# Gate and up weights turned by the host instead of folded on the chip, their low-rank term as one more product, and query blocks as 64-row products

## What is computed

```python
xn = layernorm(x)                                  # 2048 tokens, 512 wide
# attention: 32 heads of 16, 8 groups of keys and values, causal
s = softmax(mask(q @ k.T) / 4) @ v @ Wo + bo       # q = xn @ Wq, k, v = xn @ Wkv
# gated layer with low-rank terms (rank 16), hidden width 1376
gate = xn @ gate_w.T + (xn @ gate_a.T) @ gate_b.T
up   = xn @ up_w.T   + (xn @ up_a.T)   @ up_b.T
hid  = silu(gate) * up
y    = hid @ down_w.T + (hid @ down_a.T) @ down_b.T
out  = x + s * silu(y)
```

## Time and profile before

| | us |
|---|---|
| median of three runs | 944.62 |
| the profiled execution | 946.66 |
| its span, first to last instruction | 944.9 |
| TensorE busy | 896.9 (95%) |
| VectorE busy | 583.7 (62%) |
| ScalarE busy | 488.5 (52%) |
| GpSimd busy | 314.7 (33%) |
| mean granted TensorE clock | 0.984 |
| DMA | 129.20 MB, mean 137 GB/s |

### The profile page before, as it was taken

One profiled execution on the slowest core, in us unless ns is written; L12 is line 12 of the kernel. 1 busy time (PEld: TensorE's weight loads), 2 busy tenths in 40 slices (PEclk: granted clock), 3 DMA queues, 4 the chain that ended last, 5 costly groups with the idle time before them and its releaser, 6 DMA issues.

```text
span 944.9 us, 21107 instructions
## 1 busy us (share of the span) xinstructions
PE 896.9 (95%) x8075; PEld 633.1 (67%) x8075; DVE 583.7 (62%) x1688; ACT 488.5 (52%) x990; POOL 314.7 (33%) x316
## 2 busy tenths in 40 slices
PE   3898999999999999999999999999889999999997
PEld 3765667676766666667676766554667777777885
DVE  7756666666666666665656565777666666650136
ACT  3522656565555656565656565656445454546211
POOL 4231235252525343525252434441121313121133
PEclk9978999999999999999999999998999999999999
DMA  9466343333333342424242434347565647415774
GB/s 290 165 193 192 92 129 97 122 97 114 108 115 110 97 130 83 137 71 148 58 138 84 126 99 121 100 142 204 155 183 156 171 124 194 137 53 171 205 216 142
DMA packets 142946, 129.20 MB, mean 137 GB/s; under 512 B 36176, under 2 KB 104368, under 8 KB 142624
## 3 DMA queue, kind: packets, MB, share of 16 engines
q1 hardware_dynamic: 142848, 127.87, 45.6%
HBM read 74.07 MB, written 53.22 MB: 135 GB/s over the span
## 4 chain that ended last, share of the span: by engine, by line
PE 88%; DVE 5%; DMA 3%; ACT 2%; issue 2%; SPq 1%; DVEq 0%
PE bank L1011 27%; PE o L1182 14%; PE bank L1045 12%; PE s L1146 10%; PE st L1165 8%; PE bank L286 4%; PE bank L287 4%; PE bank L288 4%; DMA ring<-in_L_attn_x 2%; PE bank L986 1%; PE bank L990 1%; DMA q<-scratch_q 1%; DVE junk L1723 1%; PE s L1153 1%; ACT prob L1442 1%
## 5 line engine op out<-in xcount | busy, mean ns | idle before, releaser
L1442 ACT ACTIVATE prob<-st 128x512 f32<-128x512 f32 (+1 forms) x640 | 323.2, 554 | 263.4 <-PE st L1165 262.8
L1723 DVE CUSTOM_DVE_ANT_0 junk<-s,mask 128x128 bf16<-128x128 f32 (+3 forms) x512 | 229.1, 487 | 69.7 <-PE s L1146 67.9
L1726 DVE TENSOR_REDUCE part_max<-s 128x1 f32<-128x512 f32 x256 | 164.0, 682 | 116.3 <-PE s L1146 116.1
L1146 PE MATMUL s<-k,q 64*128 64x512 f32 (+3 forms) x768 | 150.7, 379 | 12.2 <-DVE part_max L1723 4.6
L567 POOL TENSOR_SCALAR_AFFINE_SELECT prob<-prob 128x512 f32<-128x512 f32 x128 | 81.8, 652 | 225.8 <-ACT prob L1442 224.3
L1011 PE MATMUL bank<-x_hi,w_hi 64*128 64x512 f32 (+1 forms) x704 | 150.2, 412 | 2.4 <-DVE hid L1564 1.1
L1182 PE MATMUL o<-prob,v 128*32 128x512 f32 (+3 forms) x1536 | 145.4, 497 | 0.0
L1011 PE MATMUL bank<-x_lo,w_hi 64*128 64x512 f32 (+1 forms) x704 | 142.8, 391 | 0.0
L1011 PE MATMUL bank<-x_hi,w_lo 64*128 64x512 f32 (+1 forms) x704 | 142.1, 389 | 0.0
L1165 PE MATMUL st<-q,k 64*128 64x512 f32 (+3 forms) x768 | 130.7, 356 | 2.3 <-ACT prob L1442 1.8
L1146 PEld LDWEIGHTS s<-k,q 64*128 64x128 f32 x768 | 79.1, 188 | 53.6 <-DVE part_max L1723 24.4
(11 more groups left out here) (148 smaller groups left out, 1089.0 us busy)
## 6 DMA issues: line engine op xcount, KB each, us to landing
late_context_hid_in<-scratch_hid SPq DMA_DIRECT2D x16, 1408.0 KB, 7.2
q<-scratch_q SPq DMA_DIRECT2D x60, 200.0 KB
scratch_hid<-tanh_hid_hi SPq DMA_DIRECT2D x40, 256.0 KB, 2.1
scratch_hid<-hid_lo SPq DMA_DIRECT2D x40, 256.0 KB, 2.4
scratch_o<-o_sb SPq DMA_DIRECT2D x32, 256.0 KB
scratch_q<-proj_hi SPq DMA_DIRECT2D x30, 256.0 KB
k<-scratch_k SPq DMA_DIRECT2D x30, 192.0 KB
x_again<-in_L_attn_x SPq DMA_DIRECT2D x16, 256.0 KB, 4.4
```

Source lines behind the costliest of these rows:

```text
L1146: pe.matmul(sb_[(p + odd) % S_BANKS][:, 0:wd], q[half, g % 2, h // 2, qt * P:(qt + 1) * P], k[half, g % 2, k0:k0 + wd], start=True, stop=T ...
L1442: nc.scalar.activation(prob[:, job % 3, h, 0:JOB_COLS[j]], st[at % ST_BANKS][:, 0:JOB_COLS[j]], ACT.Exp, scale=float(HD) ** -0.5).then_inc ...
L1723: ins = dve.tensor_tensor_reduce(junk[:, n % S_BANKS, 0:wd], bank_[:, 0:wd], mask[:, C - wd:C], 1.0, LOWEST, ALU.add, ALU.max, part[:, h, ...
L1726: ins = dve.tensor_reduce(part[:, h, qt, dst:dst + 1], bank_[:, 0:wd], AX.X, ALU.max)
```

## The change

- **Weights.** The host hands gate_w and up_w over turned, so that a raw tile has the layout of wh. `fold` goes. ScalarE rounds from the ring (`round_weight`), GpSimd makes the low part (`low_weight`), in the chunks 2 and 3 of the tile before; those of tile 0 right behind the last value product.
- **Low-rank term.** x times low_a is made once for all tokens (`low(0)`, `low(1)`: each 8 float32 matmuls of 32 output rows by 512 columns), split, stored to DRAM and loaded as 48 rows for gate and 48 for up (six transfers). Each of the 44 `hidden` units gets one more pair of matmuls, 48 rows each. The low part of low_b moves from VectorE (four of 32x688 elements) to GpSimd (two), that of low_a goes.
- **Query blocks.** The eleven blocks beside `hidden` are made by 64-row products with 256 columns, over both banks and 8 steps (4 for the last), and split in two halves by ScalarE and VectorE.
- **Hidden values** lie in DRAM by token tile, so that a load of one tile is one run per partition and a store has 128-column pieces. `load_hidden(2)` moves from the end of `down(0)` to the middle of `down(1)`, the loads of the first two are set apart, the low-rank pieces of down come one unit later.
- **The last turn** of the maxima is put 4 slots later.
- The counts follow: EARLY goes from 42 to 46 steps, MIDDLE and TAIL (82) stay, and the last value product now ends two steps into MIDDLE, where it ended two before.

```diff
-STEPS = dict(turn=1, proj=KT, value=TT, fold=2, hidden=2 * KT, ...)
+QUERY_STEPS = [2 * KT] * (NH - 1) + [KT]
+STEPS = dict(turn=1, proj=KT, value=TT, low=KT, hidden=2 * KT, ...)
     # order of the background (bank_order and every engine's background())
     for c, blk in LEADING: proj(c, blk)
+    low(0)
     for c in range(2): value(c)
     for c in BESIDE:
         turn(c, 0..3)
+        if c == 3: low(1)
         proj(*BESIDE[c]); proj(c, KEYS_BLOCK); value(c)
     for c, blk in AFTER[:SOON]: proj(c, blk)
-    fold(0, 0); fold(0, 1)
     for h in range(NH):
         for c in range(NCH):
             hidden(h, c)
             if c == 1:
-                if h + 1 < NH: fold(h + 1, 0); fold(h + 1, 1)
                 proj(*AFTER[SOON + h])
...
+            def low(i):                                            # TensorE
+                pe.wait_ge(xT_copied, 2 * KT * (i + 1))
+                for kt in range(KT):
+                    for c in range(2):
+                        mm = pe.matmul(out_[GROUP * c:GROUP * (c + 1), :], a_raw[:, kt], xT[:, c, kt],
+                                       start=kt == 0, stop=kt == KT - 1)
...
             def hidden(h, c):
+                        if kt == KT - 1 and not cross:
+                            if h == 0 and c == 0:
+                                pe.wait_ge(low_lo, 2)
+                                pe.wait_ge(x_a_landed, 6 * DMA)
+                            for i in range(2):
+                                at = head_rows(i, LOW_ROWS)
+                                mm = pe.matmul(bank[i][0:hp, :], b_gu[at, h * P:h * P + hp],
+                                               low_x_a[at, c * C:(c + 1) * C], start=False, stop=False)
...
             def project(c, blk):
+                if (c, blk) in BESIDE_HIDDEN:                      # the eleven of AFTER[1:]
+                    tiles = QUERY_TILES if (c, blk) != BESIDE_HIDDEN[-1] else OUT_STEPS
+                    yield from changing_over(("proj", c, blk), ..., tiles)
+                    return
...
-            def split_weight(h, i):                                # ScalarE, from the bank of the fold
+            def round_weight(h, i):                                # ScalarE, from the ring
+                if n == 0:
+                    for odd in range(2): act.wait_ge(v_stored[odd], DMA * NCH // 2)
+                    act.wait_ge(xT_lo_late, 2 * KT)
+                act.wait_ge(raw_landed[n % 8], DMA * (n // 8 + 1))
+                nc.scalar.activation(wh[:, h % 2, i, :, 0:hp], raw_tile(n)[:, :, 0:hp], ACT.Copy)
-            low_weight(h, i): dve.tensor_tensor(..., bank_of(key), ...)
+            low_weight(h, i): pool.tensor_tensor(wl[...], raw_tile(n)[...], wh[...], ALU.subtract)
...
                 # ScalarE's background, after the last value product
-                split_low_a()
+                for i in range(2):
+                    round_weight(0, i)
...
                 # VectorE's background
                 statistics(3)
                 normalise_x(3)
+                yield STEPS["low"]
+                low_of_x_a(0)
                 yield 2 * STEPS["value"]
...
     slots.append(slot)
+    slots[-1] += LAST_TURN                                         # 4: the last turn of the maxima
...
                 # SyncE
-                sp.dma_start(s["hid"][j, h, 0:rows[h], c * C:(c + 1) * C], part_...)
+                sp.dma_start(s["hid"][TT * c:TT * (c + 1), 0:rows[h], j, h].rearrange("t p n -> p t n"), part_...)
+                    if t == 1:
+                        load_hidden(2)
                     yield STEPS["down"] - LOAD_AT
-                    if t + 2 < NT:
+                    if 1 <= t < NT - 2:
                         load_hidden(t + 2)
...
             # host
+    for name in ("gate_w", "up_w"): arrays[...] = arrays[...].T
```

More of the change, by code:

```diff
@@ L101 @@
 PROJECTED = LEADING + [p for c in BESIDE for p in (BESIDE[c], (c, KEYS_BLOCK))] + AFTER
+BESIDE_HIDDEN = AFTER[1:]
+QUERY_TILES = [[[0], [1], [2], [3]]] * 2
 RAW_LOW, RAW_DOWN = 2 * NH, 2 * NH + 4
+QUERY_STEPS = [2 * KT] * (NH - 1) + [KT]
 RAWS = RAW_DOWN + NH
 REST = 2
-STEPS = dict(turn=1, proj=KT, value=TT, fold=2, hidden=2 * KT, down_fold=2, rest=REST, down=NH + 1, out=KT)
+STEPS = dict(turn=1, proj=KT, value=TT, low=KT, hidden=2 * KT, down_fold=2, rest=REST, down=NH + 1, out=KT)
 SPLIT_DOWN, SPLIT_OUT = 12, NT // 2
@@ L161, in bank_order @@
         yield "proj", c, blk
+    yield "low", 0, 0
     for c in range(2):
@@ L210, in bank_places @@
             continue
-        if kind == "hidden" or kind == "down" and a < SPLIT_DOWN or kind == "out" and a < SPLIT_OUT:
+        if kind == "hidden" or kind == "proj" and (a, b) in BESIDE_HIDDEN or kind == "down" and a < SPLIT_DOWN or kind == "out" and a < SPLIT_OUT:
             used = (0, 1)
@@ L339, in layer @@
             pl = sbuf(first, "proj_lo", [P, 2, C], F32R)
+            b_gu = sbuf(first, "low_b", [HALF_ROWS + LOW_ROWS, F], F32R)
             with ExitStack() as own:
@@ L1013, in hidden @@
                                                stop=cross == 1 and kt == KT - 1 and x_ is xl)
+                        if kt == KT - 1 and not cross:
+                            if h == 0 and c == 0:
+                                pe.wait_ge(low_lo, 2)
+                                pe.wait_ge(x_a_landed, 6 * DMA)
+                            for i in range(2):
+                                at = head_rows(i, LOW_ROWS)
+                                mm = pe.matmul(bank[i][0:hp, :], b_gu[at, h * P:h * P + hp], low_x_a[at, c * C:(c + 1) * C],
+                                               start=False, stop=False)
                         if kt == KT - 1:
@@ L1094, in background @@
                     yield from project(c, blk)
+                yield from low(0)
                 for c in range(2):
@@ L1099, in background @@
                         yield from turn_x(c, kt)
+                    if c == 3:
+                        yield from low(1)
                     yield from project(*BESIDE[c])
@@ L1104, in background @@
                     yield from project(c, blk)
-                for i in range(2):
-                    yield from fold(0, i)
                 for h in range(NH):
@@ L1110, in background @@
                         if c == 1:
-                            if h + 1 < NH:
-                                for i in range(2):
-                                    yield from fold(h + 1, i)
                             yield from project(*AFTER[SOON + h])
```

298 lines of the change are left out of this document (170 added, 128 removed).

## The result

The changed kernel took 951.91 us (median of 11 runs, 948.72 to 957.58), the kernel before 945.56 us beside it (11 runs, 942.65 to 950.45): a ratio of 1.0071, 95% interval 1.0051 to 1.0091. It is slower by more than the 0.3% that can be told, and inside the forecast's own range (941 to 953), 5 us above its centre of 946.5. Against the kernel timed beside it the change costs 6.4 us, where the forecast had 2; that it would come out slower was given 0.40. The profiled execution took 951.72 us, with a span of 950.0 (before 944.9).

What follows compares the result with a forecast made beforehand. TensorE, busy 95% of the span, was taken as the bound, with ScalarE's exponentials becoming it in the query slots. Middle -9, start +13, end -2.6 gave about +2 us on 944.6: 946.5, its own range 941 to 953.

Steps and rivals of the forecast that it cites:

- low(0): Before the hidden units: 8 added matmuls of 512 columns in two column tiles, side by side, 1.9 us.
- 48-row pairs: Hidden units, 100 to 635 us: 44 added pairs run side by side at 0.23 us each, +10.1 us.
- Query slots: Slots 22 to 30 of ten tiles: ScalarE's exponentials set the pace, 6.1 us instead of 8.0, -19 us.
- The middle: 100 to 635 us, eleven tiles: added pairs +10 and shorter query stretches -19, together -9 us (-22 to 0).
- The wait at value(1): Near 41 us: value(1) waits for the low part of x_a, behind copy, root and normalisation, 4.5 us.
- The slow stretch of 48 to 58 us: Before the hidden units: half of the 4.5 us that this half-clock stretch costs goes, -2.2 us.
- clock term: Before the hidden units: after 4.5 us without work the clock is at half, value(1) takes 3 us more.
- T to the first hidden product: Value store lands at T + 17 to T + 18, hidden starts at T + 23: +2 us, and +1 for clock.
- restart rival: Start: value store landing over 19 us after T leaves TensorE still 12 us or more; 954 us, chance 0.14.
- The six low-rank loads hidden: Start: the six x_a loads, 3 us of issue, are needed four steps into the first unit and stay hidden.
- After the hidden units: End of kernel: query-load wait -2.1, last turn's wait -1.5, low-rank piece of down +1.0; sum -2.6 us.
- start off the path: Rival: the start's new waits overlap present ones, so it costs +3 instead of +13; 936 us, chance 0.22.

Runs made afterwards that it cites:

- The edits alone: Kernel before with only the last turning of the maxima 4 slots later and hidden tile 2 loaded within down tile 1: 939.62 us, ratio 0.9946.

## Why the prediction held, step by step

The mechanism was right in its three parts and in their signs; the time was at the upper side of the range because one term, the way from T (the end of the last key product) to the first hidden product, was too small. The end of the kernel gave part of that back, by more than was forecast for it.

- **48-row pairs**, +10.1 forecast for 44: 7.3 for the 42 in the middle, by the kernel without them. Side by side as argued; a quarter of their price was hidden, of which the waits for the exponentials show 0.4 us.
- **Query slots**, 8.0 to 6.1 by the exponentials' pace: 6.4 measured, and the halved exponentials show whose pace it is. TensorE alone would need 5.25, not 4.8. The rule of the Trainium skill ("TensorEngine Tiling (Array Packing)", PSUM Bottleneck), that the emptying of banks can become the bound, agrees with the 30 stops, 7.6 us in all. Ten tiles gained 16 us where 19 were forecast. The middle came to -8.7 against -9, then, by luck: the pairs cost 3 us less and the slots gained 3 us less.
- **low(0)**, 1.9 forecast in column tiles side by side: 3.63. The mistake was in reading: a row marked x16 for `o<-prob,v` stands for eight products, two instructions each, and `low(0)` is eight products of the same float32 kind, shown as x16 too. Two side by side take 0.91 us, not 0.465. The upper end, 3.7, is the right number by the wrong reason (products in series). The same holds for `low(1)`.
- **The wait at value(1)**, 4.5: 4.48, by the path through copy, root and normalisation that the prediction gave. Its slow clock cost 2.1 (5.95 against 3.84), not 3.0.
- **The slow stretch of 48 to 58 us**: taken off by half, but gone whole; from 50 us on the clock is full. That, and the smaller clock term, paid for `low`, so T rose by 10.7 where the sum said 10.3: right for partly cancelling errors.
- **T to the first hidden product**, +2 and +1 for the clock: it was +8.3 (21.3 to 29.6). This is the step that failed. The chain was as described, down to the instruction; two of its sizes were not. The landing of the value store was put at T + 17 to T + 18, with 4.2 to 6.6 us from the earlier trace rows. None of those stores stood behind loads of that size; two came right behind group 0's, half as large. This one took 8.9 us and came at T + 21.2, past the T + 19 from which the restart rival says that it decides. And from the landing to the first hidden product 5.5 us were forecast and 8.0 measured: six products of a query block lie between the two pairs `st`, and at half clock these are 3.6 us apart (113.57 to 117.15) instead of 1.6. The stop was 14.9 us instead of ten. The result is thus the forecast's mechanism at the size of the restart rival, which was priced at 954.
- **The six low-rank loads hidden**: no wait is recorded for them. They don't hold the value store either: with the six right behind it it landed in 3.9 us when ahead of group 1's loads, and with the six ahead of those loads and none behind it in 9.1. Put first they hold group 1's loads.
- **After the hidden units**, -2.6: 2.0 - 7.2 = -5.2. Of this the +2.0, in which the added low-rank piece lies, is within what the same program varies by, so that the piece's +1.0 is neither shown nor refuted. The two waits gave more than their length: behind the query wait lay a stretch at clock 0.71 that went with it. The edits alone gave 5.1 by the medians.
- **The rival "start off the path"**, 0.22, is refuted by three kernels that shorten the start and get it back at the end.

By stretches: +19.0 where +13 was forecast, -8.7 where -9, -5.2 where -2.6; the forecast's terms add up to +1.4, which it rounded to 2, these to +5.1. Had the end given back only the 2.6 that was forecast, the time would have been about 954.5, outside the range: that it lies inside is in part luck.

## What to carry to other kernels

An operation moved by a few steps passes other operations on the queues: list what it then stands behind, and take the landing time of a transfer from a row that has as many bytes ahead of it, not from quiet ones. A wait that guards reused memory should name only the buffer it reuses; here the first rounding waited for a store whose buffer nobody wrote for another 40 us, at 8.5 us. Count a row's instructions against the program's before dividing its time, since a float32 product shows as two.

## What the runs showed of the hardware

- A 256 KB store landed in 7.4 to 10.3 us behind group 1's six loads of 1.2 MB (ten kernels), in 3.6 to 4.7 behind group 0's six loads of 0.6 MB (changed kernel and kernel before), and in 3.9 ahead of group 1's, with six smaller loads behind it.
- A long stop of TensorE costs twice: granted clock 0.53 at 46 to 50 us after 4.5 us, 0.50 at 113 to 117 after 14.9 us. Short stops among loosely fed products can do it too: 0.50 at 654 to 664 us behind a wait of 1.44, whereas the 30 stops of up to 0.3 us in the middle left it at full.
- 48-row products at rows 0 and 64 in different banks run side by side like 64-row ones, 0.24 us for 512 columns.
